# Side work of a 256-step scan cut into other pieces: states transposed from where they lie, one product a step, and a new order behind the scan

## What is computed

```python
def step(h, xt):                      # 256 steps, 8 sequences, 128 units
    m = concatenate([xt, h]) @ weight + bias
    g = sigmoid(m[:, :128] + 1.0)
    c = tanh(m[:, 128:])
    h_new = g * h + (1.0 - g) * c
x = x + scan(step, cond, x)

ada = cond @ w_ada + b_ada            # six vectors a sequence: shift, scale, gate, twice
xm = expmap0(layer_norm(logmap0(x)) * (1 + sc_msa) + sh_msa)
q, k, v = heads of plin(xm, w_q, b_q), plin(xm, w_k, b_k), plin(xm, w_v, b_v)
attn = softmax(q k^T / sqrt(8)) v     # 16 heads of 8, all 256 positions
x1 = mobius_add(x, expmap0(g_msa * logmap0(plin(attn, w_o, b_o))))
ff = plin(plin(expmap0(layer_norm(logmap0(x1)) * (1 + sc_mlp) + sh_mlp), w_f1, b_f1), w_f2, b_f2)
out = x + mobius_add(x1, expmap0(g_mlp * logmap0(ff)))
```

## Time and profile before

| | us |
|---|---|
| median of 3 runs (481.15 to 482.98) | 481.76 |
| the profiled execution | 481.39 |
| its span, first to last instruction | 479.1 |
| first tanh of the first step to first tanh of the last | 13.7 to 313.1 |
| from there to the end | 166.0 |
| PE, DVE, ACT, POOL busy, share of the span | 74%, 66%, 45%, 30% |

### The profile page before, as it was taken

One profiled execution on the slowest core, in us unless ns is written; L12 is line 12 of the kernel. 1 busy time (PEld: TensorE's weight loads), 2 busy tenths in 40 slices (PEclk: granted clock), 3 DMA queues, 4 the chain that ended last, 5 costly groups with the idle time before them and its releaser, 6 DMA issues.

```text
span 479.1 us, 14029 instructions
## 1 busy us (share of the span) xinstructions
PE 355.4 (74%) x5194; PEld 247.0 (52%) x5194; DVE 314.8 (66%) x1939; ACT 215.3 (45%) x963; POOL 143.8 (30%) x295
## 2 busy tenths in 40 slices
PE   1997988887766796768999999999489878737000
PEld 1646674665555665645666755655345445526000
DVE  5444444675887575787476577653843389999884
ACT  2224222323334324334545445555479897642440
POOL 6000000022381023282013166014610123556862
PEclk9999999999999999999999999999869998957555
DMA  7107600010000000000000000000000000000003
GB/s 177 56 1 145 123 3 1 2 47 1 2 2 3 1 2 1 1 3 3 1 3 3 1 3 2 1 4 1 2 1 3 1 1 3 2 2 0 1 0 88
DMA packets 9113, 8.41 MB, mean 18 GB/s; under 512 B 1275, under 2 KB 7693, under 8 KB 9046
## 3 DMA queue, kind: packets, MB, share of 16 engines
q1 hardware_dynamic: 8950, 7.26, 6.7%
q0 software_dynamic: 96, 0.26, 0.2%
HBM read 6.45 MB, written 1.08 MB: 16 GB/s over the span
## 4 chain that ended last, share of the span: by engine, by line
PE 50%; DVE 23%; ACT 13%; POOL 6%; issue 6%; DMA 1%; SPq 0%; DVEq 0%; POOLq 0%; ACTq 0%
PE zb L791 19%; PE tb L896 5%; PE tb L742 4%; DVE prod_hi L1410 4%; PE zb L770 4%; ACT prd L1290 3%; ACT state L1157 3%; PE firsts L939 3%; DVE prod_lo L1416 3%; PE firsts L960 2%; PE firsts L1032 2%; POOL stat L692 2%; ACT state L1160 2%; PE zb L776 2%; PE firsts L791 2%
## 5 line engine op out<-in xcount | busy, mean ns | idle before, releaser
L791 PEld LDWEIGHTS zb<-prod_hi,whh 128*128 128x128 f16 x1920 | 73.5, 106 | 94.3 <-DVE prod_hi L1410 86.9
L791 PE MATMUL zb<-prod_hi,whh 128*128 128x8 f16 x1920 | 90.7, 171 | 40.4 <-DVE prod_hi L1410 39.3
L1157 ACT ACTIVATE state<-zb 128x8 f32<-128x8 f32 x240 | 42.6, 178 | 167.5 <-PE zb L791 167.5
L1410 DVE SCALAR_TENSOR_TENSOR prod_hi<-state 128x16 f16<-128x16 f32 x255 | 47.4, 186 | 97.7 <-ACT state L1160 95.1
L791 PE MATMUL zb<-prod_lo,whh 128*128 128x8 f16 x960 | 63.3, 172 | 2.6 <-DVE prod_lo L1416 0.9
L1416 DVE TENSOR_TENSOR prod_lo<-prod,prod_hi 128x16 f16<-128x16 f32 x255 | 50.6, 199 | 8.7
L791 PEld LDWEIGHTS zb<-prod_lo,whh 128*128 128x128 f16 x960 | 44.2, 106 | 6.1 <-DVE prod_lo L1416 3.1
L599 POOL TENSOR_TENSOR stat<-mv 128x4 f32<-128x4 f32 x4 | 0.8, 206 | 154.9 <-DVE mv L1505 154.9
L1412 DVE SCALAR_TENSOR_TENSOR prod<-state 128x16 f32<-128x16 f32 x256 | 43.3, 169 | 0.5 <-ACT state L1160 0.5
L1290 ACT ACTIVATE prd<-zb 128x640 f32<-128x640 f32 x64 | 40.9, 718 | 4.3 <-PE zb L1011 4.1
L1160 ACT ACTIVATE state<-zb 128x16 f32<-128x16 f32 x240 | 42.7, 178 | 0.0
(11 more groups left out here) (322 smaller groups left out, 716.3 us busy)
## 6 DMA issues: line engine op xcount, KB each, us to landing
mod<-ada_rows SPq DMA_DIRECT2D x4, 768.0 KB, 12.3
resid<-in_x_dram SPq DMA_DIRECT2D x6, 128.0 KB, 3.6
ffz<-shift_rows SPq DMA_DIRECT2D x4, 131.0 KB, 3.2
out_dram<-state SPq DMA_DIRECT2D x8, 64.0 KB, 2.1
out_dram<-early SPq DMA_DIRECT2D x8, 64.0 KB, 2.1
yy<-in_L_cond_w_ada_dram SPq DMA_DIRECT2D x1, 384.0 KB
early<-in_L_cond_weight_dram SPq DMA_DIRECT2D x2, 128.0 KB
resid<-in_x_dram POOLq DMA_DIRECT2D x2, 128.0 KB, 3.6
```

The costliest lines, as they stand in the source:

```text
L791: i = pe.matmul(z_bank(t, k)[:, NB * (t % CH):NB * (t % CH) + NB], whh[:, half, p, k, :], src[:, NB * p:NB * p + NB], start=False, stop=Fa ...
L1157: act.activation(r[:, 24:32], z_bank(t, 1)[:, k:k + NB], ACT.Tanh, scale=-1.0 / ZS)
L1410: dve.scalar_tensor_tensor(prod_hi[:, :], r[:, 16:32], 1.0, r[:, 0:16], ALU.add, ALU.mult).then_inc(hi_ready, 1)
```

## The change

1. ACT's copy of the states (`hcopy`, line 1209) is gone. PE reads `state` itself: for each pair of sequences two products with the identity, 64 columns of `state` at the pitch of 96 bytes as the stationary operand, one into the upper and one into the lower 64 partitions of the bank. During the scan one such pair stands in each of four ticks.
2. In `prepare`, PE's products for `ada` stand one a tick instead of two, ACT's four instructions on `ada` one a tick, the transposes of x two a tick instead of four, and the row product with 257 columns is split in two. The transposes of `w1` come before those of x. The later ticks move back by about ten.
3. For the first three chunks POOL no longer normalizes and modulates sequences 0 and 1: ACT normalizes all four (two instructions in each of two ticks), DVE modulates all four (four instructions in four ticks).
4. Everything behind the transposes in a chunk stands two ticks later. Two semaphores are split for the last tail (`att_sq_last`, `ff_sq_last`).
5. `TOK_LAST`, the tails' tables and `DIAG` have new numbers, so the order behind the scan is another.

The diff, cut to its core:

```diff
 TOK = dict(
-    hcopy=0, transpose=1, resid=3, moments=5, norm=8, artanh=10, rho=17, xn=19, modulate=21,
+    transpose=1, resid=5, moments=7, norm=10, artanh=12, rho=19, xn=21, modulate=23, utrans=26,
...
 TOK_LAST = dict(
-    hcopy=20, transpose=35, resid=54, moments=62, norm=75, artanh=96, rho=143, xn=159,
+    transpose=22, resid=42, moments=50, norm=63, artanh=85, rho=130, xn=146, modulate=155,
...
 # POOL, tokens
-                    pool.wait_ge(tok_rho, c + 1)
-                    yield from at_ticks(now, base + T["xn"])
-                    if c:
+                    if c == NC - 1:
+                        pool.wait_ge(tok_rho, c + 1)
+                        yield from at_ticks(now, base + T["xn"])
                         pool.wait_ge(tok_uT_ps, c)
...
 # PE, x_transposes
                     i = transpose(xT_bank(c)[:, D * j:D * j + D], resid[:, NJ * c + j, :], identf)
+                    if c and j == 1:
+                        yield
                 i.then_inc(xT_ps, 1)
+                yield
 # PE, prepare
                                   start=(q == 0), stop=False, skip_group_check=True)
+                        yield
                         i = pe.matmul(tb[0:NB, h, 128 * q:128 * q + 128], ones[:, 0:NB],
...
                 for k in range(4):
-                    i = pe.matmul(ob[0:1, 0:2 * D + 1], ffw[:, k, 2 * D:2 * D + 1], ffw[:, k, :],
-                                  start=(k == 0), stop=(k == 3))
-                    yield
+                    for cols in (slice(0, D), slice(D, 2 * D + 1)):
+                        i = pe.matmul(ob[0:1, cols], ffw[:, k, 2 * D:2 * D + 1], ffw[:, k, cols],
+                                      start=(k == 0 and cols.start == 0), stop=(k == 3),
+                                      skip_group_check=True)
+                        yield
 # PE, tokens
-                    pe.wait_ge(h_copied, c + 1)
+                    pe.wait_ge(step_in, 2 * CH * (c + 1) + (1 if c < NC - 1 else 0))
                     for j in range(NJ):
-                        i = transpose(tb[:, 0, D * j:D * j + D], tus[:, j, :], identf)
-                        if j == 1:
+                        for s in range(2):
+                            h = state[:, SW * (CH * c + 1) + batch_of(c, j, s):][:, 0:1]
+                            i = pe.matmul(tb[CH * s:CH * s + CH, 0, D * j:D * j + D], view(h, [SW, CH]), identf[:, :],
+                                          start=(j == 0), stop=True, skip_group_check=True)
+                        if j == 1 or T is TOK and j < NJ - 1:
                             yield from part(now, base, T, "transpose")
 # ACT, prepare
-                    yield from at_ticks(now, 17 + 3 * c)
+                    yield from at_ticks(now, 26 + 4 * c)
                     copy_xT(c)
-                yield from at_ticks(now, 43)
+                yield from at_ticks(now, 37)
                 act.wait_ge(w1T_ps, 1)
 # ACT, tokens
-                    yield from at_ticks(now, base + T["hcopy"])
-                    act.wait_ge(step_in, 2 * CH * (c + 1) + (1 if c < NC - 1 else 0))
...
-                    for j in (2, 3):
+                    for j in (2, 3, 0, 1) if c < NC - 1 else (2, 3):
+                        if j == 0:
+                            yield
 # DVE, tokens
+                    if c < NC - 1:
+                        yield
+                        dve.wait_ge(tok_xn, 2 * c + 2)
+                        done_(dve.tensor_tensor(tu[:, 0:2, :], tu[:, 0:2, :], mod[:, c & 1, 0:2, D:2 * D],
+                                                ALU.mult))
+                        mark = done[0]
+                        yield
+                        settle(mark)
+                        dve.tensor_tensor(tu[:, 0:2, :], tu[:, 0:2, :], mod[:, c & 1, 0:2, 0:D],
+                                          ALU.add).then_inc(tok_u, 1)
```

More of the change, by code:

```diff
@@ new lines @@
+    wosq=(1091,), asq=(3574,), adot=(1101,), norm=1111, tanh=1141, mob=1144, ascale=(1163,),
+    root=1176, x2=(1175,), v=(1187,), vtrans=(1199,), vevac=(1218,), vsq=(1223,), artanh=1198,
+    lin=(1285,), rho=1301, t6=(1250,), g=(1263,), gy=(1301,), gdot=(1300,), usum=1317,
+    clip2=1358, fq=1335, e=(1353,), f1=1377, clip3=1392, y=(1391,), f2=(1411,), f2sq=(1423,),
+    ffsq=(4126,), fdot=(1431,), norm3=1441, fftanh=1468, mob2=1480, ffscale=(4214,),
+    out=(1526,), add=(4254,), artanh_=(1203, 1205, 1207, 1210, 1213, 1215, 1217, 1219, 1223,
@@ L703, in work @@
                     pool.wait_ge(wo_sq, last + 1)
-                    pool.wait_ge(att_sq, last + 1)
+                    if last < NJ - 1:
+                        pool.wait_ge(att_sq, last + 1)
+                    else:
+                        pool.wait_ge(att_sq_last, 1)
+                        if len(pairs) > 1:
+                            pool.wait_ge(att_sq, last)
                     vector_norms("a").then_inc(att_n, 1)
@@ L723, in work @@
                     pool.wait_ge(f2_sq, last + 1)
-                    pool.wait_ge(ff_sq, last + 1)
+                    if last < NJ - 1:
+                        pool.wait_ge(ff_sq, last + 1)
+                    else:
+                        pool.wait_ge(ff_sq_last, 1)
+                        if len(pairs) > 1:
+                            pool.wait_ge(ff_sq, last)
                     vector_norms("f").then_inc(ff_n, 1)
@@ L819, in prepare @@
                 i.then_inc(ada_ps, 1)
-                for c in range(1, NC):
-                    yield from at_ticks(now, 16 + 3 * c)
-                    x_transposes(c)
-                yield from at_ticks(now, 27)
-                yield from x_part(1)
                 for k in range(4):
@@ L829, in prepare @@
                 i.then_inc(w1T_ps, 1)
-                yield from at_ticks(now, 45)
+                for c in range(1, NC):
+                    yield from at_ticks(now, 24 + 4 * c)
+                    yield from x_transposes(c)
+                    if c == 1:
+                        x_part_1 = x_part(1)
+                    else:
+                        for _ in range(2):
+                            next(x_part_1)
+                            yield
+                yield from x_part_1
+                yield from at_ticks(now, 46)
                 pe.wait_ge(w1T_sb, 1)
@@ L847, in prepare @@
                 transpose(ob[:, 0:NB], ada[:, 3 * D:4 * D], identf).then_inc(shT_ps, 1)
-                yield from at_ticks(now, 63)
+                yield from at_ticks(now, 74)
                 pe.wait_ge(shT_sb, 1)
@@ L1178, in prepare @@
                     .then_inc(w1T_sb, 1)
-                yield from at_ticks(now, 58)
+                yield from at_ticks(now, 65)
                 act.wait_ge(gw_ps, 1)
@@ L1183, in prepare @@
                 act.activation(gwrow[:, :], ob[0:1, D:2 * D + 1], ACT.Copy).then_inc(gw_sb, 1)
[L1184 removed]
+                yield from at_ticks(now, 71)
                 act.wait_ge(beta_ps, 1)
@@ L1189, in prepare @@
                 act.activation(shT[:, :], ob[:, 0:NB], ACT.Copy).then_inc(shT_sb, 1)
-                yield from at_ticks(now, 67)
+                yield from at_ticks(now, 77)
                 act.wait_ge(shift_ps, 1)
```

174 lines of the change are left out of this document (85 added, 89 removed), and 6 rows, old and new, of the table scores.

## The result

The changed kernel takes **473.9 us** (median of four runs, 473.87 to 477.10) where the kernel before takes 481.5; the ratio is 0.985, 95% interval 0.981 to 0.990. Measured a second time beside the experiments it was 0.9854 (0.9836 to 0.9871). The profiled execution took 473.87 us, span 472.0. The forecast was 476.7, range 472.2 to 481.2.

A forecast was written before the change was run, and what follows sets the result against it. The loop PE, ACT, DVE, PE bounds the scan at 1.062 us a step; behind it, a dependent chain. Scan gain 9.36 - 4.80 = 4.56 plus tail 0.5 takes 481.39 to 476.33; 0.37 for the median gives 476.7 us, range 472.2 to 481.2.

The forecast's parts named there:

- products for `ada`, steps 12 to 17: Early scan: one PE product a tick instead of two makes six steps plain, gaining 2.39 us.
- ACT's `ada`: Step 18: four ACT instructions spread over four steps fit in ACT's 0.81 us idle time, gaining 0.36 us.
- state copies: Scan, first three chunks: dropping ACT's 1.48 us copy gains 3.27 us, before the cost of what replaces it.
- POOL's modulation: First three chunks: without POOL's instructions DVE's `prod_lo` is no longer held, gaining 0.71, 0.71 and 0.35, together 1.77 us.
- lone pairs: Steps 65 to 68 and 129 to 131: seven pairs alone in their step cost 0.15 us each, 1.05 together.
- step 132: The eighth pair shares its step with the first `x_part` product, costing 0.40 us as two 32-bit products do.
- steps 193 to 196: Third chunk: four pairs, each beside a group of scores or values, cost 0.50 us each, 2.0 together.
- step 253: Near the scan's end: three groups of attention work and two exponentials in one step cost 0.40 us (0 to 0.8).
- tail: Behind the scan: shorter chain and new order together gain 0.5 us, bounds 3 gained to 2.3 lost.
- the quartet: Step 195: four products in four column groups, eight passes, take 0.64 us; so a pair's cost of 0 is possible.
- The new order costs what its tick numbers say: Rival, behind the scan: tail ends 2.3 us later instead of 0.5 earlier, 479.5 us; chance 0.17.
- The two rivals on the pairs: Pairs: strided weights paid in full, 480.8 us, chance 0.10; or no overlap within a pair, 484.9 us, chance 0.07.

The follow-up runs named there:

- a2: Changed kernel with POOL's normalization and modulation of two of the four tiles back in the first three chunks: 476.3 us, 0.988 of the kernel before.
- b1: Changed kernel with seven local edits, each aimed at a long step left in the scan: 471.3 us, 0.981 of the kernel before.
- b3: Changed kernel with ACT's copy and four plain transposes back in the last chunk alone: 474.6 us, 0.987 of the kernel before.
- a4: Changed kernel with all six old order tables for what stands behind the scan, pairs kept: 477.7 us, 0.990 of the kernel before.
- a3: Changed kernel with pairs reading 64 neighbouring columns instead of a pitch of 96 bytes (computation altered): 474.3 us, 0.985 of the kernel before.
- a1: Changed kernel with ACT's states copy and PE's four plain transposes back in the first three chunks: 476.6 us, 0.988 of the kernel before.
- d2: b1 with the last chunk's pairs put first, and tiles 2 and 3 in another bank so DVE's sum splits: 470.7 us, 0.978 of the kernel before.
- d3: d2 with ACT's copy and plain transposes back in the third chunk alone: 470.7 us, 0.978 of the kernel before.
- b2: Changed kernel with the old `TOK_LAST` and `DIAG` numbers, the four tails keeping the new ones: 480.7 us, 0.999 of the kernel before.
- b4: Changed kernel with the old numbers for the first tail alone (`TAIL0`): 483.3 us, 1.006 of the kernel before.
- d0: The changed kernel again, unedited, five runs on the same chip: median 475.1 us, 0.985 of the kernel before.

## Why the prediction was right, and where it was wrong

Term by term, in us gained:

| term | forecast | measured |
|---|---|---|
| products for `ada`, steps 12 to 17 | 2.39 | 1.95 |
| ACT's `ada` | 0.36 | 0 (0.35 in step 18, back in 26) |
| x transposes | 0.38 | 0.38 |
| 257-column product | 1.19 | 1.19 |
| state copies | 3.27 | 3.26 |
| POOL's modulation | 1.77 | 1.62 (a2) |
| lone pairs | -1.05 | 0 |
| step 132 | -0.40 | -0.63 |
| steps 193 to 196 | -2.0 | -2.18 |
| steps 38, 76, 80 | -0.95 | -0.98 |
| step 253 | -0.40 | -0.78 |
| scan | 4.56 | 3.62 (the terms give 3.83; 0.2 is spread over other steps) |
| tail | 0.5 | 3.45 |

The reading of single steps held in the main: the six terms taken away came to 8.4 of 9.36 us, each within 0.45, though one of them (ACT's `ada`) to nothing.

- *The lone pairs* were mis-sized: "I take 0.15 us a pair", measured 0. The lower bound from the quartet was the truth, since the pair's 0.71 us end inside the gap.
- *"One a tick is what steps 27 and on have for nothing"* overlooked that in step 13 another engine was late too: 0.44 us of DVE work that the two products had hidden.
- *ACT's `ada`*: that spread over four steps they "fit" overlooked ACT's wait for its own copy. In the kernel before the four instructions did outlast step 18 (they end at 36.49 us; a plain step has the next tanh at 36.25). One a tick, the wait alone costs as much in step 26, and with the wait moved it costs nothing (b1).
- *Step 132* and *step 253* had the right mechanism and the wrong size, since I took the price of two products in a step and not the sum of the durations: 0.77 + 0.71, and in 253 PE's values that wait for an exponential.
- *The tail* failed as a step: "I take 0.5 gained, near the middle". The measured 3.45 lies outside my bounds (3 gained), and 2.95 from the forecast, just under the 3 us that I had named as a sign of being wrong. The chain, "the only thing that a row shows", gives 0.4 us at DVE's sum, with the four pairs at 2.0 us instead of my 1.6 (b3, without it, ends 0.75 later); a4 gives the order 3.5 in the profiles, 2 at the least by the executions' times. *The new order costs what its tick numbers say* had the wrong sign: the last output stands 22 numbers later and came 2.6 us sooner. A number that orders one engine's list isn't a time, even where it had gone in step with one.
- The two rivals on the pairs are refuted by the steps 65 to 68 and by a3.

- *The change's first item* brought almost nothing by itself: the copies' 3.26 us went, and the pairs took 2.8 of them back; a1 puts the difference at 0.3 us of the scan.

So the direction was right for the reasons given in the scan. That the time came out within the range was in part luck: a scan gain too large by 0.9 met a tail gain too small by 3, and the larger part of that was an order whose gain no row had shown.

The best kernels measured are d2 and, level with it, d3 (470.7 both). d2, the seven edits with the pairs first and the sum split, is at 0.978 of the kernel before (0.976 to 0.980), below the changed kernel's 0.9854 (0.9836 to 0.9871) in the same series.

## What to carry to other kernels

In a loop with a fixed slack per step, add up the durations of all that one engine does in a step, its waits for itself included, and compare the sum with the gap. Here b1 took nine long steps back to plain, each by what had been read off it. When a stall is removed, look for the second engine that was late in the same step. The numbers of a hand-made order can't be read as times. Halves of two orders may not fit together (b2 and b4 were slower than either whole order), so an order is priced by swapping it whole. Before a difference behind a busy stretch is explained, compare the granted clock of both profiles there.

## What the runs showed of the hardware

- The first 64-column FP32 weight load of a pair takes 201 ns at a pitch of 96 bytes against 180 to 183 from neighbouring columns (a3). ACT's copy of 512 columns of `state` at that pitch takes 1.48 us, its copy of 512 neighbouring columns out of the PSUM tile `firsts` 0.61; no run changes the pitch alone.
- Two products on two column halves start 7 ns apart, and in four pairs in a row (eight passes on each half) both halves begin a pass every 0.21 us.
- ACT waiting for its own copy ahead of the loop's wait costs 0.37 us, though the copy had ended 0.3 us before PE's last product began.
- The same kernel on the same chip ran from 473.6 to 476.8 us. A profile of 476.82 (d0) and one of 473.87 (the first series) differ by a fall of PE's clock to 1.2 GHz behind 385 us, in stretches of 5 us in which PE was busy for 4.2 to 5.0 us.
